# Stack operands of sixteen-dimensional attention heads loaded by six requests instead of eight

## The reference

```python
q = (x @ Wq.T + bq).reshape(B, S, 16, 16).transpose(0, 2, 1, 3)   # k and v alike
scores = jnp.einsum('bhqd,bhkd->bhqk', q, k) / math.sqrt(16)
out = jnp.einsum('bhqk,bhkd->bhqd', softmax(scores), v)
```

## Time and profile before

| what | value |
|---|---|
| runs shown | 4847.12, 4855.64 and 4861.48 us, median 4855.64 us |
| profiled execution | 4844.51 us, span 4842.7 us |
| mean granted clock of PE | 0.909 of full speed |
| PE busy | 4152.1 us, 86% |
| DVE busy | 2875.1 us, 59% |
| ACT busy | 2348.2 us, 48% |
| POOL busy | 1359.4 us, 28% |
| DMA | 332041 packets, 486.56 MB, mean 100 GB/s |

### The profile page before, as it was taken

The page is one execution under the profiler, slowest core; times in us unless marked ns, Lnnn a source line. Parts: engine busy times, 40 slices in busy tenths (PEclk is TensorE's granted clock), DMA queues, the critical chain, the costliest instruction groups (busy, mean ns, idle before and its releaser), DMA issues. The chain is left out here.

```text
span 4842.7 us, 69706 instructions
## 1 busy us (share of the span) xinstructions
PE 4152.1 (86%) x20384; PEld 1973.3 (41%) x20384; DVE 2875.1 (59%) x6517; ACT 2348.2 (48%) x4572; POOL 1359.4 (28%) x1202
## 2 busy tenths in 40 slices
PE   8679866689788997797998999999998888489986
PEld 6322355377453233484233333333335554222224
DVE  4458573501667885203863378787873256388876
ACT  4337331243234775243664455454552236379993
POOL 0121141212101111101220188787883212101112
PEclk9669987799888999798898999999999899789998
DMA  8545212354133332574335521111110134523421
GB/s 289 116 99 125 63 39 35 115 203 154 45 110 85 66 67 64 202 257 152 82 77 199 183 77 62 62 62 62 62 59 1 45 107 103 142 63 94 101 52 38
DMA packets 332041, 486.56 MB, mean 100 GB/s; under 512 B 84516, under 2 KB 232596, under 8 KB 317252
## 3 DMA queue, kind: packets, MB, share of 16 engines
q1 hardware_dynamic: 321552, 443.63, 32.1%
q0 software_dynamic: 6384, 32.61, 2.1%
q10 hardware_dynamic: 3804, 6.74, 0.4%
HBM read 327.63 MB, written 143.92 MB: 97 GB/s over the span
## 5 line engine op out<-in xcount | busy, mean ns | idle before, releaser
L1406 POOL TENSOR_TENSOR lc_totals<-lc_totals,lc_weights 128x1024 f32<-128x1024 f32 (+1 forms) x320 | 623.0, 1947 | 164.1 <-DVE lc_totals L1355 133.7
L1336 DVE TENSOR_REDUCE lc_part_max<-ps 128x2 f32<-128x1024 f32 x384 | 466.3, 1214 | 218.3 <-PE ps L1181 215.9
L1315 ACT ACTIVATE lc_weights<-ps 128x1024 f32<-128x1024 f32 x384 | 393.1, 1024 | 415.9 <-PE ps L1201 402.7
L1201 PE MATMUL ps<-lc_q,lc_k 64*128 64x512 f32 x1536 | 395.3, 593 | 4.3 <-issue 4.3
L1211 PE MATMUL ps<-lc_weights,lc_v 128*64 128x512 f32 x1536 | 371.7, 605 | 0.0
L876 DVE TENSOR_REDUCE l1x_core_part_max<-ps 128x1 f32<-128x512 f32 x512 | 318.6, 683 | 59.2 <-PE ps L697 58.2
L872 DVE CUSTOM_DVE_ANT_0 l3x_core_unused<-ps,l3x_core_mask_q 128x512 f32<-128x512 f32 x512 | 331.9, 686 | 9.8 <-DVE l3x_core_row_max L880 5.9
L835 ACT ACTIVATE l3x_core_weights<-ps 128x512 f32<-128x512 f32 x512 | 329.0, 698 | 9.9 <-PE ps L764 5.9
L835 ACT ACTIVATE l1x_core_weights<-ps 128x512 f32<-128x512 f32 x512 | 266.2, 603 | 87.1 <-PE ps L764 87.1
L818 ACT ACTIVATE ps<-l3x_core_mask_k 128x512 f32<-128x512 f32 x384 | 272.3, 709 | 34.9 <-DMA l3x_core_mask_k<-in_mask_k 34.9
L697 PE MATMUL ps<-l3x_core_k,l3x_core_q 96*128 96x512 bf16 x512 | 210.4, 412 | 47.8 <-DVE l3x_core_part_max L872 29.5
(11 more groups left out here) (494 smaller groups left out, 8572.7 us busy)
## 6 DMA issues: line engine op xcount, KB each, us to landing
cf_w<-in_L1f_w SPq DMA_DIRECT2D x32, 1024.0 KB, 8.0
lc_k<-latent_k SPq DMA_DIRECT2D x32, 768.0 KB
lc_v<-latent_values SPq DMA_DIRECT2D x32, 768.0 KB, 4.9
latent_k<-feed_staged SPq DMA_DIRECT2D x64, 256.0 KB
latent_values<-feed_staged SPq DMA_DIRECT2D x64, 256.0 KB
k_heads<-proj_parts SPq DMA_DIRECT2D x40, 384.0 KB, 2.6
q_heads<-proj_parts SPq DMA_DIRECT2D x32, 384.0 KB, 2.6
q_heads<-proj_parts SPq DMA_DIRECT2D x32, 256.0 KB, 3.0
```

Source lines behind the costliest of these rows:

```text
L1201: mm = nc.tensor.matmul(out[j], k_tile[g % RING][strip(j), i * P:(i + 1) * P], q_tile[g % RING][strip(j), :], start=False, stop=True)
L1315: nc.scalar.activation(weights[:, i % TILES, :, :], k.ps[:, B0 + (i % 2) * HEADS:B0 + (i % 2 + 1) * HEADS, 0:nq], ACT.Exp, scale=scale).th ...
L1336: nc.vector.reduce_max(own, k.ps[:, A0:A0 + HEADS, :], AX).then_inc(a_taken, 1)
L1406: nc.gpsimd.tensor_tensor(total, total, own, ALU.add).then_inc(added_by_pool, 1)
```

## The change

The six products are taken in another order. The query stack's blocks are now high, high, high, mid, low, mid; the key stack's high, mid, low, high, high, mid. With that order a stack is three requests: for the queries the high part repeated three times (a source with a leading dimension of 3 and stride 0), mid and low together (32 rows), mid (16 rows); for the keys the three parts (48 rows), the high part repeated twice (a leading dimension of 2 and stride 0), mid (16 rows). So a group is loaded by six requests, 192 rows as before. Queries are stored like keys, one DRAM tensor of three slots, one request of 384 KB a unit. In l3a_core the slopes' request stays, seven instead of nine. The class for the third layer's cross-attention (`ChannelParts`) and its stores are untouched.

```diff
--- before.py
+++ after.py
@@ -285,26 +285,30 @@
 class HeadParts:
 
 
-
-
     HEADS = P // HD
-
-    def __init__(self, nc, name, slots, n):
-        self.n = n
-        self.parts = [nc.dram_tensor(f"{name}{i}", [B, CH, s, HD, self.HEADS, n], BF16, kind="Internal").ap() for i, s in enumerate(slots)]
+    ROWS = {"q": ((0, 3, 1), (1, 1, 2), (1, 1, 1)), "k": ((0, 1, 3), (0, 2, 1), (1, 1, 1))}
+
+    def __init__(self, nc, name, which, n):
+        self.n, self.which = n, which
+        self.parts = nc.dram_tensor(name, [B, CH, 3, HD, self.HEADS, n], BF16, kind="Internal").ap()
 
     def rows(self, m, t, width):
 
         b, first = divmod(t * width, self.n)
-        return tuple(part[b, m, :, :, :, first:first + width].rearrange("s d h n -> (d h) s n") for part in self.parts)
+        return (self.parts[b, m, :, :, :, first:first + width].rearrange("s d h n -> (d h) s n"),)
 
     def loads(self, stack, b, g):
 
         heads = slice(g % 2 * HG, (g % 2 + 1) * HG)
-        own = [part[bass.ds(b, 1), g // 2, :, :, heads, :] for part in self.parts]
-        out = [(stack[0:3 * HD, :, :], own[0].rearrange("o s d h n -> (o s d) h n"))]
-        for i, slot in enumerate(Q_OTHERS if len(own) == 2 else K_OTHERS):
-            out.append((stack[(3 + i) * HD:(4 + i) * HD, :, :], own[-1][:, slot, :, :, :].rearrange("o d h n -> (o d) h n")))
+        own = self.parts[bass.ds(b, 1), g // 2, :, :, heads, :]
+        out, row = [], 0
+        for slot, repeated, taken in self.ROWS[self.which]:
+            rows = stack[row * HD:(row + max(repeated, taken)) * HD, :, :]
+            if repeated > 1:
+                out.append((rows, own[:, slot].rearrange("o d h n -> (o d) h n").unsqueeze(0).broadcast_to((repeated, HD, HG, self.n))))
+            else:
+                out.append((rows, own[:, slot:slot + taken].rearrange("o s d h n -> (o s d) h n")))
+            row += max(repeated, taken)
         return out
 
 
@@ -1640,7 +1644,7 @@
         place = {1: 0, 2: 256, 3: 384}
         bias = sb("bias", [P, 4, 3 * CH])
         vbias = sb("vbias", [P, 4, CH])
-        q_coarse, k_coarse = HeadParts(nc, "q_coarse", (3, 2), S), HeadParts(nc, "k_coarse", (3,), S)
+        q_coarse, k_coarse = HeadParts(nc, "q_coarse", "q", S), HeadParts(nc, "k_coarse", "k", S)
         v_coarse = nc.dram_tensor("v_coarse", [B * 4, P, H * QUAD], F32, kind="Internal").ap()
         q_parts, k_parts, values = k.q_heads, k.k_heads[S], k.values
         xs = k.xT[:].rearrange("p c (b s) -> p c b s", b=B)
@@ -3058,7 +3062,7 @@
         k.head_blocks, k.head_cols = sb("head_blocks", [P, P]), sb("head_cols", [P, CH, H])
         k.q_parts = tuple(nc.dram_tensor(f"q_parts{i}", [C, slots, T], BF16, kind="Internal").ap() for i, slots in enumerate((3, 2)))
         k.k_parts = (nc.dram_tensor("k_parts", [C, 3, TC], BF16, kind="Internal").ap(),)
-        k.q_heads, k.k_heads = HeadParts(nc, "q_heads", (3, 2), S), {n: HeadParts(nc, f"k_heads_{n}_", (3,), n) for n in (S, SC)}
+        k.q_heads, k.k_heads = HeadParts(nc, "q_heads", "q", S), {n: HeadParts(nc, f"k_heads_{n}", "k", n) for n in (S, SC)}
         k.values = nc.dram_tensor("values", [NT, P, H * QUAD], F32, kind="Internal").ap()
         k.slots_in = nc.dram_tensor("slots_in", [2 * T, C], F32, kind="Internal").ap()
         k.slots_out = nc.dram_tensor("slots_out", [2 * T, C], F32, kind="Internal").ap()
```

## The result

The changed kernel took 5104.86 us in the median (5098.63 to 5107.19) against 4854.91 us: 1.0521 of the time before, 95% interval 1.0507 to 1.0536. It is slower by 250 us where +127 was forecast. The time lies just inside the stated range (up to 5110), the sign and the crowded DMA engines were as forecast, and the size is twice what the sum gave. So the question is which terms were too small.

A forecast was written before the change was run, and what follows sets the result against it. The prediction took what stands ahead of the maxima row in SP's queue to set pyr_coarse's pace. 71 + 25 + 41 - 10 = +127 us on the profiled 4844.5 gave 4971, on the median 4983; forecast 4980, range 4838 to 5110.

The forecast's parts named there:

- idle time in the loops: Steady groups, 12 a stage, wait for later maxima: pyr_coarse +23, pyr_core +26, l2a_core and l3a_core +11 each, l1x_core 0; +71 us.
- PE's lower clock: After waits over a boundary PE's clock drops, 1.7 us lost each: pyr_core 20, l2a_core and l3a_core 5; +25 us.
- starts: Four groups of loads before each stage's first maxima row: five starts take 176.5 us instead of 135.7, +41 us.
- the price of a row on the crowded engines: Stack loads: a 4 KB row takes 0.187 us at 22 GB/s an engine, so 39 rows take 7.3 us.
- the time at which l2a_core's and l3a_core's rows were due: l3a_core's maxima row due 8.91 us after T0, the value load's issue; +0.9 us a group, l2a_core given the same.
- Spread of a request: Stack loads: outermost dimension sets the engine count, so repeats run on 3 and 2, the busiest taking 39 rows.
- Rivals C and D: Stack loads: C, repeats on different engines, 4833 us, chance 0.04; D, one request per copy, nine a group, 4852 us, 0.05.
- rival B: Stack loads: repeats flattened to 48 and 32 rows over 16 engines; -30 us, 4826 us, chance 0.11.
- single store: Projections: queries stored once, 384 KB instead of 384 + 256 KB; a third of VectorE's 31.7 us wait saved, -10 us.
- What stands behind what: DMA queues: the maxima's last bytes queue behind 39 rows on two crowded engines, row at 10.6 us after the value load's issue.

The follow-up runs named there:

- e1_spread: The changed kernel with the 16 head dimensions outermost in every request, slot or copy inside; 4835.68 us, 0.9976 of the kernel before.
- e3: The changed kernel with only the query repeat narrow, the keys' repeat as two requests of 16 rows; 4945.86 us, 1.0201 of the kernel before.
- e4: The changed kernel with only the key repeat narrow, the queries' repeat as three requests of 16 rows; 4930.60 us, 1.0173 of the kernel before.
- e5_start_spread: The changed kernel with each stage's first four groups loaded by nine requests, each copy its own; 5045.02 us, 1.0412 of the kernel before.
- e2_nine: The changed kernel with every copy of a repeat as its own 16-row request, nine a group; 4853.36 us, 1.0016 of the kernel before.
- e6: The changed kernel with the maxima requests issued after one load request, the five other loads behind them; 5243.32 us, 1.0811 of the kernel before.
- e7: The kernel before with the three maxima requests issued after one load request, the seven other loads behind them; 4918.82 us, 1.0142.

## Why the prediction was right in kind and wrong in size

Against the terms of the sum the traces have: idle time in the loops 142 us for 71, PE's lower clock 70 for 25, starts 58 for 41, the rest of the kernel -10 for -10; together 260 for 127. Most of the miss is in l2a_core and l3a_core, whose loops grew by 52 and 54 us where the sum had 11 each and a share of 5 for the clock. The steps that failed are the price of a row on the crowded engines (0.187 us taken, 0.21 measured over a whole transfer), the time at which l2a_core's and l3a_core's rows were due, and the clock behind their waits.

- **Spread of a request.** Right: the four-partition store of the earlier trace rows was the right row to lean on. Shares of 0.18 and 0.12, and e1_spread, show it; e3 and e4 show that the two repeats share engines. Rivals C and D are out, and rival B is what e1_spread made of the change, worth 11 us and not 30.
- **Price of a row on one engine**, the first term that failed. 39 rows and the values' 4 were to take 7.3 + 0.8 = 8.1 us at 22 GB/s an engine. In pyr_coarse bytes move from about 163.2 to 172.3, 9.1 us, 0.21 us a row. I had taken one rate for the whole transfer, near the fast end of the earlier trace rows. The tail does run at 24.5 GB/s an engine, 0.167 us a row. At that rate, by my estimate, some 26 of the 43 rows fall in the 4.3 us behind 168, and the other 17 took the 4.8 us before it, 0.28 us each. That first part, with all engines at work, is slower than the earlier trace rows, and in it the crowded engines get little ahead of the others, which had 11 rows' worth. Why that part is so slow no run separates.
- **The due time**, the second. For l3a_core I took 8.91 us from a group that was already late by 1.52, and gave l2a_core the same. The changed kernel's l2a_core group, SP and PE:

```profile
2510.19 1.70 SPq L573 DMA_DIRECT2D l2a_core_q<-q_heads  x3
```

```profile
2521.47 0.39 PE L768 MATMUL ps<-l2a_core_q,l2a_core_k 99*128 99x512 bf16 x1 [2.71 <-DMA l2a_core_q<-l2a_core_max_parts]
```

  The row comes 11.28 us after the first load, not 9.8, which is the row's price again; without the wait of 2.71 it was due at 8.57. In l3a_core, by the earlier trace rows, it was due 7.39 us after the first load, the 8.91 less the 1.52. So in the 12 groups of the loop l2a_core waits 36.2 us, 3.0 each, and l3a_core 44.6, 3.7 each, where it had 9.3 in 5; 0.9 a group more was in the sum. Together with the row's price this is the waits' miss. l1x_core, at nothing in the sum, was 11 us longer, half in two waits at its maxima and half in PE's busy time; why was not looked into.
- **The clock**, the third: PE's busy time is 70 us longer in the loops (21 in pyr_core, 23 in l3a_core, 16 in l2a_core) against 25 in the sum. For pyr_core the term was right (20). For l2a_core and l3a_core it hung on the wait of 0.9 us staying under a boundary between 1.69 and 1.83 us. Their waits were longer; and there is no such boundary in the length of a wait. Another l2a_core wait of the changed kernel, and the 7 us behind it and behind the one shown above:

```profile
2491.59 0.39 PE L768 MATMUL ps<-l2a_core_q,l2a_core_k 99*128 99x512 bf16 x1 [2.65 <-DMA l2a_core_q<-l2a_core_max_parts]
```

```profile
2491.59:2498.59 7.00, 7.00 (x33) 2.02 (x33) 4.64 (x9) 4.49 (x9) 1.43 (x4) 0.76 0.08 23
...
2521.47:2528.47 7.00, 7.00 (x39) 2.48 (x40) 5.91 (x11) 5.40 (x11) 1.91 (x4) 1.00 0.22 40
```

  Behind 2.65 us the granted clock was 0.76 in the mean, behind 2.71 it stayed at 1.00. Of l2a_core's 12 waits in the loop nine were followed by 0.58 to 0.76, and three (2.35, 2.48 and 2.71 us) by 1.00. What decides between them these runs don't show. That pyr_core's term came out was in part luck: it was priced by one wait.
- **The starts**: +58 us by the traces, 53 or 54 by e5_start_spread, against +41; each start was 2 to 6 us longer than forecast, which is the row's price again. The **single store**: outside loops and starts the changed kernel is 10 us shorter, as forecast, but the traces of e1_spread and e2_nine give 1 and 11, so this agreement may be luck. VectorE's wait for the stores did shrink, from 31.7 to 14.3 us, while waiting for ScalarE grew, 78.7 instead of 69.4; its idle time before the cast fell from 120.1 to 104.0:

```profile
L262 DVE CAST proj_parts<-proj_full 128x512 bf16<-128x512 f32 x88 | 37.5, 426 | 104.0 <-ACT proj_full L223 78.7 <-DMA q_heads<-proj_parts 14.3 <-DMA k_heads<-proj_parts 7.1
```

- **What stands behind what.** The prediction had the maxima queue behind the narrow rows and called that the new wait. The loads ahead of them are due at the same time, so the sum, which counts to the last byte, did not suffer from it; but I had not looked when the loads are due, and the expectations of e6 and e7 went the wrong way for it.

## What to carry to other kernels

Count what a request puts on its busiest DMA engine, not its bytes: a leading dimension of 2 or 3 made a narrow request here, and turning the same access inside out, with 16 rows outermost, took back 5%. Before moving a transfer within a queue, find for each transfer in it the first instruction that reads what it brings; a load "three groups ahead" was due within one. When a change puts waits of 2 to 4 us into every group, cost the clock for every stage that gets them, and don't draw a boundary from two waits. Take the due time from a group that is not late already.

## What was not expected of the hardware

Fewer requests were not fewer microseconds of issue: six requests of 16 to 48 rows took 3.75 us in e1_spread, eight, six of them of 16 rows, 3.79; the form of the access counted (0.42 or 0.58 us), not the rows. And a crowded engine reaches back to the issuing engine. SP's timeline at the start of pyr_coarse in the changed kernel:

```profile
116.87 1.85 SPq L573 DMA_DIRECT2D pyr_coarse_q<-q_coarse  x3
...
126.47 6.84 SPq L573 DMA_DIRECT2D pyr_coarse_q<-q_coarse  x3
```

Three requests took 6.84 us to issue behind two groups with narrow rows and two value loads, where the first three took 1.85; the longest single one, in pyr_core, took 8.1 us. By this, what waits in front of the crowded engines can hold SP up, and with it everything that SP has to issue. In e5_start_spread, whose starts have no narrow request, the longest issue of a query load in these two stages takes 0.9 us; in the kernel before the longest in pyr_coarse takes 1.1.
